# Layer 2 of a gated cross-attention network: value products moved between units, the mix one unit later

## What is computed

```python
# for one sequence: x are its tokens, ctx its context
ln = layernorm(layernorm(x)) * gamma_lat + beta_lat     # (512, 128)
xn = layernorm(ctx) * gamma_media + beta_media          # (77, 128)
q = (ln @ Wq + bq) * 128 ** -0.5                # 8 heads of 128
k, v = split(concat([xn, ln]) @ Wkv + bkv)      # 77 + 512 = 589 keys
out = softmax(q @ k.T) @ v                      # per head
x = x + tanh(g_xattn) * (out @ Wo + bo)
```

## Time and profile before

| | |
|---|---|
| median of 3 runs | 1539.65 us (1536.65 to 1540.21) |
| profiled execution | 1535.79 us, its span 1533.6 us |
| TensorE busy | 1393.0 us, 91% of the span |
| VectorE busy | 805.6 us, 53% |
| ScalarE busy | 756.1 us, 49% |
| GpSimd busy | 124.2 us, 8% |
| mean granted TensorE clock | 0.978 of full |
| layer 2's units | 167 to 382 us in the first pass, 922 to 1137 us in the second |

### The profile page before, as it was taken

The page is one execution under the profiler, slowest core; times in us unless marked ns, Lnnn a source line. Parts: engine busy times, 40 slices in busy tenths (PEclk is TensorE's granted clock), DMA queues, the critical chain, the costliest instruction groups (busy, mean ns, idle before and its releaser), DMA issues.

```text
span 1533.6 us, 26446 instructions
## 1 busy us (share of the span) xinstructions
PE 1393.0 (91%) x8788; PEld 1129.2 (74%) x8788; DVE 805.6 (53%) x2147; ACT 756.1 (49%) x1622; POOL 124.2 (8%) x115
## 2 busy tenths in 40 slices
PE   6987899999999987899979888999999998888999
PEld 5685567777898765679947756677779887566898
DVE  4693544554434747753357825445543456476532
ACT  2752455555543454554447425555554434545443
POOL 1042000000000002000011410000000100020000
PEclk9999999999999999999989999999999999999999
DMA  5002000000002000000000020000000020000000
GB/s 199 1 1 111 1 1 1 1 2 1 1 1 93 18 1 1 6 1 15 1 16 1 1 110 1 1 2 1 1 1 2 1 111 1 1 1 1 1 8 8
DMA packets 4038, 27.88 MB, mean 18 GB/s; under 512 B 1054, under 2 KB 1344, under 8 KB 2880
## 3 DMA queue, kind: packets, MB, share of 16 engines
q1 hardware_dynamic: 3184, 22.55, 3.7%
q10 hardware_dynamic: 720, 3.59, 0.6%
HBM read 25.09 MB, written 1.05 MB: 17 GB/s over the span
## 4 chain that ended last, share of the span: by engine, by line
issue 69%; PE 18%; DVE 7%; POOL 3%; ACT 2%; DMA 0%; DVEq 0%; SPq 0%; POOLq 0%; ACTq 0%
PE psum L659 16%; DVE nmax L1345 2%; DVE rsum L1354 1%; POOL rs L1201 1%; PE psum L693 1%; POOL arenaD L1216 1%; ACT arenaB L994 1%; POOL x L1228 1%; DVE arenaA L1572 1%; ACT arenaA L994 1%; DVE xn L1300 1%; DVE psum L1341 0%; DMA mask<-in_mask_dram 0%; DVE x L1377 0%; DVE arenaA L1570 0%
## 5 line engine op out<-in xcount | busy, mean ns | idle before, releaser
L659 PEld LDWEIGHTS psum<-moe,arenaA 128*128 128x128 f32 x2048 | 239.2, 194 | 8.3 <-issue 1.9
L659 PE MATMUL psum<-moe,arenaA 128*128 128x128 f32 x2048 | 241.6, 277 | 2.2 <-DVE gt L1454 1.4
L994 ACT ACTIVATE arenaB<-psum 128x512 f32<-128x512 f32 x448 | 168.2, 428 | 115.7 <-PE psum L693 114.9
L659 PE MATMUL psum<-arenaD,arenaB 128*128 128x128 f32 (+2 forms) x1440 | 190.8, 281 | 13.2 <-ACT arenaB L994 12.6
L994 ACT ACTIVATE arenaA<-psum,vec 128x512 f32<-128x512 f32 (+1 forms) x208 | 125.3, 613 | 156.6 <-PE psum L659 156.4
L659 PEld LDWEIGHTS psum<-arenaD,arenaB 128*128 128x128 f32 (+1 forms) x1440 | 173.7, 193 | 25.6 <-issue 11.2
L1425 DVE CUSTOM_DVE_ANT_0 probs<-psum,shift 128x589 f32<-128x589 f32 x128 | 98.7, 771 | 166.5 <-PE psum L659 164.4
L994 ACT ACTIVATE probs<-probs,nmax 128x589 f32<-128x589 f32 x128 | 100.8, 787 | 170.9 <-DVEq L1428 170.9
L1402 DVE SCALAR_TENSOR_TENSOR x<-psum,gt,x 128x128 f32<-128x128 f32 x256 | 72.0, 344 | 213.7 <-PE psum L659 213.7
L693 PE MATMUL psum<-w_first,probs 128*128 128x128 f32 (+2 forms) x1120 | 160.6, 274 | 8.1 <-POOL probs L1240 3.1
L659 PE MATMUL psum<-parts 128*128 128x512 f32 x672 | 166.4, 397 | 0.0
(11 more groups left out here) (200 smaller groups left out, 1767.6 us busy)
## 6 DMA issues: line engine op xcount, KB each, us to landing
moe<-in_w_moe_dram SPq DMA_DIRECT2D x4, 4096.0 KB, 12.8
moe<-in_w_folds_dram SPq DMA_DIRECT2D x3, 1024.0 KB, 9.7
w_l<-in_w_l_dram ACTq DMA_DIRECT2D x1, 1372.0 KB, 12.7
x<-in_x_dram SPq DMA_DIRECT2D x4, 256.0 KB, 4.0
out_dram<-x SPq DMA_DIRECT2D x4, 256.0 KB, 2.1
w_rest<-in_w_rest_dram ACTq DMA_DIRECT2D x1, 768.0 KB, 8.9
w_first<-in_w_first_dram ACTq DMA_DIRECT2D x1, 596.0 KB, 5.3
w_second<-in_w_second_dram ACTq DMA_DIRECT2D x1, 512.0 KB, 6.6
```

What stands on the lines that cost most here:

```text
L659: return nc.tensor.matmul(out, lhsT, rhs, start=start, stop=stop, skip_group_check=shared)
L994: return nc.scalar.activation(out, in_, func, **kw)
```

## The change

Only `schedule()` changes; no step is added, removed or resized. The ten value products and the shift product of s = 1 go into a list `rest`. `norm_turn` of s = 1 comes at k = 9 instead of 8. From then on, in each iteration whose k % 4 is 1 or 2 (the second and third unit of a head), one of the list is given out: value products at k = 10, 13, 14, 17, 18, 21, 22, 25, 26 and 29, the shift product at k = 30. Queries products stay where they are (k % 4 = 0). The mix of a unit comes four iterations after its scores instead of three, and with it `heads_out(0)` goes from k = 35 to 36 and `heads_out(1)` from k = 67 to 68.

```diff
-    n, half = len(units), H1 * NT
+    n, half, rest = len(units), H1 * NT, values1(1) + [("shifts1", 1)]
...
-        if k == half // 4:
+        if k == half // 4 + 1:
             do("norm_turn", 2, 1, spare(k))
-        if 0 <= k - half // 4 - 4 < 10:
-            do(*values1(1)[k - half // 4 - 4], spare(k))
-        if k == half // 4 + 14:
-            do("shifts1", 1, spare(k))
-        if k == half + 3:
+        elif k > half // 4 and k % NT in (1, 2) and rest:
+            do(*rest.pop(0), spare(k))
+        if k == half + 4:
             do("heads_out", 0, G1)
...
-        if 3 <= k < n + 3:
-            do("mix_values1", *units[k - 3], k - 3, (G1, G0)[units[k - 3][0]])
+        if 4 <= k < n + 4:
+            do("mix_values1", *units[k - 4], k - 4, (G1, G0)[units[k - 4][0]])
...
-        if k == n + 3:
+        if k == n + 4:
             do("heads_out", 1, G0)
```

## The result

| | before | after |
|---|---|---|
| median of the runs compared | 1538.72 us (1536.65 to 1540.21, 4 runs) | 1517.42 us (1515.00 to 1522.89, 4 runs) |
| ratio, with its 95% interval | | 0.9871 (0.9846 to 0.9896) |
| profiled execution, its span | 1535.79 us, 1533.6 us | 1522.89 us, 1520.7 us |
| mean granted clock in it | 0.978 | 0.976 |

The change is worth 1.3%, 16.0 to 23.7 us by the interval. The direction was right, the size was not.

What follows compares the result with a forecast made beforehand. TensorE, busy 1393.0 of 1533.6 us, was taken as the bound, with only its excess in layer 2's attention removable. Terms of 6.1 us per pass, 12.2 in two, took 1539.65 to 1527.5 us; range 1522 to 1535.5.

Steps and rivals of the forecast that it cites:

- start, units 3 to 7: Layer 2 attention's first units: TensorE's waits partly go, though VectorE is late itself; 0.5 us gained per pass, between 0 and 1.5.
- norm_turn, units 8 and 9: Unit 8: queries product no longer waits for the seen copy once norm_turn moves to unit 9; 1.3 us gained per pass.
- collisions, units 10 to 30: Units 12, 16, 20: value and queries products no longer share slot G0 in one unit; 3 x 0.73 = 2.2 us gained.
- heads_out, unit 36: Unit 36: queries product waits for G1 until VectorE's later heads_out empties it; 1.6 us lost per pass, between 1.2 and 2.8.
- units 48 and 49: Units behind VectorE's gates: mixes no longer wait for late ScalarE copies; 1.2 us gained per pass, between 0.8 and 1.25.
- the other units from 37 on: Units 37 and 61: last two mix waits, 0.2 us each, and restarts go; 0.6 us gained, between 0.2 and 0.7.
- tail: Behind the last scores: mixes no longer come straight behind their turns; 1.9 us gained per pass, at least 1.2.
- the price list: TensorE prices in layer 2 attention: queries 0.86, value product 0.80, scores 1.04, mix 1.22, turn 0.55 us; plain unit 2.80.
- Rival 1: Turns at T0 and T1 wait as long as mixes did; only 3.8 us gained, 1535.9 us; chance 0.12.
- Rival 2: Clock falls behind the new wait in unit 36, costing 3.3 us per pass; 5.6 us gained, 1534.1 us; chance 0.13.
- Rival 3: heads_out is quicker than thought and the start gives back all; up to 15.3 us gained, 1524.4 us; chance 0.06.
- Rival 4: Turns at T0 and T1 wait in every unit, 128 units; at 0.24 us each 1558 us, slower; chance 0.05.

Runs made afterwards that it cites:

- lag-only kernel: Kernel before with only the mix and both heads_out one iteration later, value products as before: 1525.81 us, 0.9924 of the kernel before.
- turn-first kernel: Value products moved as in the change, mix lag kept at three, each mix put behind its iteration's turn: 1517.04 us, 0.9869 of the kernel before.
- the change again: The changed kernel unaltered, run again against the kernel before: 1517.18 us (6 runs), 0.9880 of the kernel before.
- heads_out early: The change with heads_out(0) in iteration 35, directly behind mix(31), ahead of softmax1(36): 1512.51 us, 0.9850 of the kernel before.
- only the values moved: Kernel before with value products, norm_turn and shift product moved as in the change, mix and heads_out unmoved: 1528.43 us, 0.9942 of the kernel before.

## Why the prediction was right in direction and wrong in size

What each step was to give per pass, and what unit starts before and after gave. One mix less stands ahead of scores(63) now; its 1.22 us are taken off the first line and put to the tail.

| term | forecast | measured |
|---|---|---|
| start, units 3 to 7 | 0.5 | 0.3 |
| norm_turn, units 8 and 9 | 1.3 | 1.4 |
| collisions, units 10 to 30 | 2.2 | 2.7 |
| units 31 to 35 | 0 | 0.3 |
| heads_out, unit 36 | -1.6 | -1.7 |
| units 48 and 49 | 1.2 | 1.2 |
| the other units from 37 on | 0.6 | 1.8 |
| tail | 1.9 | 2.3 |
| sum | 6.1 | 8.4 |

**The step that failed** is the price list at its beginning: "In these TensorE goes from one product to the next", "mix 1.22", and "Whatever a unit takes beyond them is excess, and excess is all that the change can take away". The plain unit of 2.80 us had an excess of its own. Its mix began 0.06 us behind the copy of its own weights, where the profile flags no wait, and the first weight load had no cover. With the copies made a unit ahead it is 1.16 us and the unit 2.75, and behind a turn or a value product 1.12. The trace of the kernel before had both: unit 23 took 250.10 - 247.35 = 2.75 us, and the mixes behind value products 214.77 - 213.66 = 1.11 (below). I took 2.75 beside 2.80 for scatter, and it was the two cases. The price of 0.80 us for a value product hid it too: that product takes 0.86 to 0.91 us by its own starts, and the unit came out at 2.80 + 0.80 since its mix was the short one. The long mix stands in 41 of the 64 units, is 0.05 to 0.1 us too long in each, and makes most of the 2.3 us per pass that the forecast lacked: 0.5 in units 10 to 30, 0.3 in 31 to 35, about 1.0 in the plain and queries units after 36, and 0.4 in the tail. The lag-only kernel, 4.8 us where I had 2.6, puts it in the lag, and the turn-first kernel, with 3.0 us of waits at turns and a stage as short, shows that the mix and not only its flagged waits got shorter.

Those rows of the kernel before, its timeline of TensorE:

```profile
213.66 1.28 PE L659 MATMUL psum<-arenaA,arenaB 128*128 128x128 f32 x10
214.77 0.71 PE L693 MATMUL psum<-w_first,probs 128*128 128x128 f32 x5
...
247.35 1.20 PE L659 MATMUL psum<-seen,qh 128*128 128x512 f32 x4
...
250.10 1.09 PE L659 MATMUL psum<-seen,qh 128*128 128x512 f32 x3
```

**The steps that held.** The collisions, norm_turn, and units 48 and 49 came as forecast; value products next to a queries product cost nothing. The new wait on heads_out is flagged 1.47 us and costs 1.7. The chain that I built for it (minimum, scaling, emptying, 0.05 us to go on) is in the rows above, step for step. The start gave 0.3 of the 0.5. Where I had said that nothing between 2.80, 3.60 and 3.66 would be seen up to unit 35, from unit 10 on 2.75 and 3.56 to 3.61 are what stands there (3.65 with the shift product): a sign wrong in size for the same reason. I had also written that I would be wrong if turns showed waits on arenaB. Two do, and the start term had itself reckoned with one of them; that sign and the term contradict each other.

**The time.** 16.8 us in the stage, 1.9 us of clock between the passes and 1.4 us of clock behind the second make 20.1, within the interval of both comparisons (16.0 to 23.7, and by that of the change again, 0.9861 to 0.9898 of 1537, 15.7 to 21.4). The 1.4 us are seen in two of the three executions of each. Of 10 us by which the forecast was off, 4.6 are the stage's, most of it the shorter mixes, and 3.3 that clock, for which the sum had no term; my base accounts for 0.9, since the median of before fell from 1539.65 to 1538.72 in the runs compared. The remaining 1.2 us I can't assign: single executions of one kernel spread over 8 us, and the start alone moves by 4.7. Nor is it shown what in the change moves the clock: these 3.3 us came unforeseen, and they stay unexplained.

**The rivals.** Rival 1 (the waits move to the turn) is shown by two turns with 0.9 us, at the start, where I had granted most; in its pure form, turn first, it is real and still faster than I forecast, since it also makes the mix short. Rival 2 (the clock falls at the new wait) didn't happen: behind 1.47 us the grant stays 1.00 in the stage, in three executions. That the Trainium skill, page "TensorE: Matmul & The Clock Gate", section "HAM oscillation — how this bites in real kernels", lets bursts parted by idle time begin slow is borne out only at the longer wait outside, and not each time: one and the same 2.31 us gave 0.59, 0.79 or 1.00, and before, which had 0.59 in the first pass, had 1.00 in the second. The price of 3.3 us that rival 2 took from that row was thus the highest seen, not the usual one. Rival 3's time, 1524.4 us, was nearer than mine, but neither of its reasons held: the wait on heads_out cost 1.7 and not 1.2, and the start gave 0.3 and not 1.5. Rival 4 (turns wait everywhere) is refuted by the waits: two of 64. Its counter-argument holds with more room than I gave it: by the earlier trace rows the copies end 196.82 - 195.54 = 1.28 us ahead of the turn, not 1.1.

**The better version** is the change with heads_out(0) behind mix(31) in iteration 35: 0.9850 (0.9828 to 0.9872) of before, 1512.51 us, 4.7 us under the change in the same group.

## What to carry to other kernels

Before pricing a removed wait, compare like with like: the shortest instance of a group in the trace is its price, and if the usual one is 0.05 us longer, look whether its weights are produced just ahead of it, because the profile need not flag a wait there: here 41 of 64 units paid it, 33 of them without one. Moving a consumer a step later helps the steps around it and delays the slot that it frees; move the emptying of the slot ahead of the long work on its engine in the same edit. A difference in the total beyond that of the stage should be looked for in the grants of several executions, and of both passes, before it is credited to the edit.

## What was unexpected in the hardware

- A mix (10 records, weights from ScalarE's copies) takes 1.22 us when the copy ends 0.06 us ahead of it, 1.16 behind a scores product when it ends 0.11 us ahead or more, and 1.11 to 1.12 behind a turn or a value product with the copies long ready. Its first weight load starts with the matmul in the first case, and 0.07, 0.11 and 0.43 us ahead behind scores, turn and value product.
- Behind one and the same wait of 2.31 us, in code that no experiment touched, the granted clock over 8 us was, in the first pass, 0.59, 0.59 and 0.60 in the kernel before, 0.79 three times in the change, and 1.00 three times with only the values moved; lag only and turn first had 1.00 too, heads_out early 0.79. In the second pass of the same executions it was 1.00 three times before, and in the change and with only the values moved 0.79 in some and 1.00 in others. The length of the wait doesn't decide it, nor does the kernel alone. What does stays open.
- In the first 40 us, which are the same in all kernels, the grant varied between executions from 0.79 to 0.91, and the first scores product stood between 171.7 us (at 0.79) and 166.9 us (at 0.91).
